# Layer 1 attention: the engines behind TensorE take the results of the projections two probability tiles later

## The reference

```python
xn = (x - mu) * rsqrt(var + EPS) * ln_g + ln_b
q = _split_heads(xn @ Wq)
kv = xn @ Wkv
k, v = _split_heads(kv[..., :INNER]), _split_heads(kv[..., INNER:])
mem = _split_heads(memories @ Wm)          # memories = the context
k = jnp.concatenate([k, mem], axis=2)
v = jnp.concatenate([v, mem], axis=2)
dots = jnp.einsum('bhid,bhjd->bhij', q, k) * scale
attn = jax.nn.softmax(dots, axis=-1)
out = jnp.einsum('bhij,bhjd->bhid', attn, v)
return out.transpose(0, 2, 1, 3).reshape(b, n, h * d) @ Wo + bo
```

## Time and profile before

| | us |
|---|---|
| median of 3 runs | 5270.39 |
| lowest and highest of them | 5267.61, 5272.48 |
| span of the profiled execution | 5269.8 |
| TensorE busy in it | 4827.1 |
| VectorE busy | 4327.4 |
| ScalarE busy | 3096.7 |
| GpSimd busy | 1940.9 |

### The profile page before, as it was taken

The page is one execution under the profiler, slowest core; times in us unless marked ns, Lnnn a source line. Parts: engine busy times, 40 slices in busy tenths (PEclk is TensorE's granted clock), DMA queues, the critical chain, the costliest instruction groups (busy, mean ns, idle before and its releaser), DMA issues. The chain is left out here.

```text
span 5269.8 us, 74714 instructions
## 1 busy us (share of the span) xinstructions
PE 4827.1 (92%) x26357; PEld 1891.5 (36%) x26366; DVE 4327.4 (82%) x4358; ACT 3096.7 (59%) x6111; POOL 1940.9 (37%) x1522
## 2 busy tenths in 40 slices
PE   8938999999999999999995699999998699999997
PEld 5623454544545454544442222222222322222222
DVE  7648878788787878878886699999996599999996
ACT  3313454454545454444442288888886288888886
POOL 0014878787787878787783100000000100000000
PEclk9968999999999999999997699999998699999998
DMA  1024334242333334142210211111110211111110
GB/s 36 5 89 117 95 92 112 60 124 51 103 81 98 98 82 122 40 123 64 51 38 15 78 29 29 29 34 29 29 23 2 78 28 29 28 29 33 30 23 6
DMA packets 171375, 298.10 MB, mean 57 GB/s; under 512 B 39061, under 2 KB 108577, under 8 KB 167393
## 3 DMA queue, kind: packets, MB, share of 16 engines
q1 hardware_dynamic: 169420, 292.95, 21.8%
q10 hardware_dynamic: 1584, 0.37, 0.0%
HBM read 187.39 MB, written 101.25 MB: 55 GB/s over the span
## 5 line engine op out<-in xcount | busy, mean ns | idle before, releaser
L1858 DVE TENSOR_REDUCE a_mx<-ps 128x1 f32<-128x1024 f32 x1536 | 1814.5, 1220 | 71.0 <-PE ps L1692 54.5
L1800 ACT ACTIVATE a_prob<-ps 128x512 f32<-128x512 f32 (+1 forms) x3264 | 1699.7, 601 | 288.1 <-PE ps L1680 283.3
L1227 POOL TENSOR_TENSOR tot_p<-tot_p,prob 128x512 f32<-128x512 f32 (+1 forms) x922 | 1300.4, 1410 | 401.5 <-ACT prob L1103 315.3
L1103 ACT ACTIVATE prob<-ps 128x512 f32<-128x512 f32 (+1 forms) x1512 | 801.1, 608 | 866.1 <-PE ps L979 865.2
L1151 DVE TENSOR_REDUCE mx<-ps 128x1 f32<-128x1024 f32 x896 | 1047.3, 1214 | 222.4 <-PE ps L956 222.4
L1692 PE MATMUL ps<-a_K,a_Q 59*128 59x512 bf16 (+1 forms) x3328 | 1094.7, 386 | 56.4 <-DMA a_Q<-q_stack_dram 44.5
L1680 PE MATMUL ps<-a_Q,a_K 59*128 59x512 bf16 (+1 forms) x3264 | 988.7, 383 | 55.8 <-ACT a_prob L1800 49.5
L1716 PE MATMUL ps<-a_prob,a_V 128*9 128x512 f32 x6528 | 871.8, 596 | 10.9 <-ACT a_acc L1784 10.9
L978 PE MATMUL ps<-QA,KA 128*128 128x512 f32 (+1 forms) x1888 | 841.7, 446 | 0.0
L990 PE MATMUL ps<-prob,V 128*64 128x512 f32 x3024 | 801.1, 599 | 0.7 <-ACT prob L1103 0.7
L979 PE MATMUL ps<-QB,KB 128*128 128x512 f32 (+1 forms) x1888 | 746.1, 395 | 0.0
(11 more groups left out here) (415 smaller groups left out, 3772.8 us busy)
## 6 DMA issues: line engine op xcount, KB each, us to landing
a_K<-k_stack_dram SPq DMA_DIRECT2D x128, 300.2 KB
k_hi_dram<-hi_s SPq DMA_DIRECT2D x112, 256.0 KB, 2.2
k_lo_dram<-lo_s SPq DMA_DIRECT2D x112, 256.0 KB, 2.4
KA<-k_hi_dram SPq DMA_DIRECT2D x64, 384.0 KB, 4.3
KA<-k_lo_dram SPq DMA_DIRECT2D x64, 384.0 KB, 5.6
KB<-k_hi_dram SPq DMA_DIRECT2D x64, 384.0 KB, 6.6
k_bf_dram<-bf_s SPq DMA_DIRECT2D x112, 128.0 KB, 1.8
KM<-k_bf_dram SPq DMA_DIRECT2D x32, 448.0 KB
```

The lines of the kernel that those rows point to most:

```text
L1103: nc.scalar.activation(prob_of(u, t)[0:r, :], c.banks(n % 3)[0:r, :], ACT.Exp, scale=SCALE).then_inc(exped, 1)
L1227: nc.gpsimd.tensor_tensor(tot_p[0:r, u % 2, :], tot_p[0:r, u % 2, :], p, ALU.add).then_inc(totalled_p, 1)
L1800: nc.scalar.activation(prob[0:r, batch % 2, t % BATCH, :], c.banks(n % 3)[0:r, :], ACT.Exp, scale=SCALE).then_inc(exped, 1)
L1858: nc.vector.tensor_reduce(mx[:, u % 2, j, i % FULL:i % FULL + 1], c.banks(slot(step), 2), AX.X, ALU.max).then_inc(maxed, 1)
```

## The change

A second constant says behind which score tile ScalarE, VectorE and GpSimd take an extra's result. TensorE and SyncE keep `EXTRAS_BEHIND`.

```diff
-    EXTRAS_BEHIND = (3, 5)
+    EXTRAS_BEHIND, TAKEN_BEHIND = (3, 5), (5, 7)
@@ block.scalar
                         for n, tile in enumerate(scored_in(u, r)):
                             exponential(*tile)
-                            if n in EXTRAS_BEHIND and extras:
+                            if n in TAKEN_BEHIND and extras:
                                 take_extra(*extras.pop(0))
```

## The result

The changed kernel takes 5445.48 us (median of 4 runs, 5442.41 to 5447.15) against 5271.43 us for the kernel before (4 runs): a ratio of 1.033, with a 95% interval of 1.0316 to 1.0345. It is 174 us slower. The forecast was 5421.5 us in a range of 5388 to 5460.

The account below looks back on a forecast made before the run. TensorE was taken to bound layer 1; stalls of 81.8 + 48.7 + 8.1 + 7.0 + 5.5 = 151.1 us on the 5269.8 us span, with 0.6 for the runs' median, gave 5421.5 us, range 5388 to 5460.

Parts of the forecast that it names:

- What bounds the kernel: Layer 1 goes at TensorE's pace: time added to its queue adds to the end; ScalarE has room.
- Two k: 56 rounds with two key projections: second maximum step of part 1 starts 1.46 us late, 81.8 us in all.
- The chain of the second step: Two-k rounds: exponentials 6 and 7, then `round_hi`, `cut_lo`, TensorE's second maximum step at 772.31 instead of 770.85.
- Two v: 42 rounds with two v projections: ScalarE's `take_v` alone releases the slot; stall 1.16 us each, 48.7 us in all.
- A fin and a v: 7 rounds with a fin, then a v behind n = 7: stall 1.16 us each, 8.1 us in all.
- One k: 7 rounds with one k, taken behind n = 5 instead of n = 3: 1.0 us each, 7 us in all.
- Fin alone: 24 rounds with only a fin: ScalarE's later `take_fin` delays TensorE's last pair 0.23 us each, 5.5 us in all.
- nothing wins it back: No TensorE work queued behind the waiting maximum step can slip past, so each stall is paid in full.
- No gain: ScalarE no longer waits for projections between exponentials, but exponential 6 starts with its score either way: no gain taken.
- That rival's 5447 us: VectorE's sum of n = 6 waits out another GpSimd sum in one k round in three: adds 26 us; chance 0.12.
- the clock: TensorE's clock falls behind the new stalls, 105 rounds' weighing at half clock: adds 389 us, 5811 us; chance 0.03.
- signs of being wrong: Second step not held, VectorE sums holding `cut_lo` in most rounds, or layer 1's granted clock under 1.

Follow-up runs that it names:

- the fill: Changed kernel with the first maximum step of part 1 issued six times in rounds with two k, keeping TensorE busy through the wait: 5414.90 us.
- ScalarE alone late: Changed kernel, but only ScalarE takes extras behind n = 5 and 7; VectorE and GpSimd as in the kernel before: 5434.96 us.
- the split kernel: Second maximum step of part 1 put behind the weighing's first four tiles: changed kernel 5311.41 us; the kernel before with the same edit 5288.00 us.
- VectorE and GpSimd alone late: Changed kernel, but only VectorE and GpSimd take extras behind n = 5 and 7; ScalarE as in the kernel before: 5347.45 us.
- k alone late: Changed kernel, but only k extras are taken two tiles later; v and fin as in the kernel before: 5389.62 us.

## Why the prediction was right, and where it was off

*What bounds the kernel: right.* ScalarE, VectorE and GpSimd all got more idle time, and the time followed TensorE's queue. Rounds without extras kept 9.22 us in every kernel of the table.

*Two k: right, with one part missing.* Worked out were 1.46 us of stall; with the clock held up by the fill, these rounds are 1.48 us longer, 83 us in all against 81.8. The chain of the second step was right link by link, and ScalarE is its longest part, as the run with ScalarE alone late shows. What it left out is the first step's wait of 0.22 us, which is hidden here but was the larger part of what the split kernel still lost.

*Two v: mis-sized.* 1.16 us was forecast, 1.00 measured (42 against 48.7 us). The step most at fault is the 0.14 us from the release to TensorE's start, borrowed from `cut_lo`. After `take_v` it is 0.05, which is 0.09 of the 0.16 us. TensorE and ScalarE in one round:

```profile
711.26 0.39 PE L956 MATMUL ps<-KM,QM 64*128 64x512 bf16 x2
712.51 0.39 PE L956 MATMUL ps<-KM,QM 64*128 64x512 bf16 x2 [0.87 <-ACT V L1063]
```

```profile
710.90 1.08 ACT L1103 ACTIVATE prob<-ps 128x512 f32<-128x512 f32 x2 [0.26 <-PE ps L979]
711.87 0.59 ACT L1063 COPY V<-ps 128x512 f32<-128x512 f32 x1
```

`take_v` ends at 711.87 + 0.59 = 712.46, and TensorE starts at 712.51. Of the rest, 0.03 us is that the two exponentials start that much sooner (0.36 us ahead of the first step, 710.90 to 711.26, in place of 0.33); and in seven of the 42 rounds the steps of part 1 stood 0.3 us later to begin with, so they lose 0.73 us and pull the mean down. The waits listed for `take_v` came to 35.0 and 5.4 us where some 50 were forecast. A fin and a v came to 0.94 against 1.16 us.

*One k: right in size,* 0.99 against 1.0 us.

*Fin alone: right in size, by the wrong cause.* These rounds are 0.23 us longer, which is the figure of the prediction, but it ascribed it to ScalarE's later copy. With ScalarE alone late the second step of part 1 is indeed held, and the weighing starts 0.15 us later. Still the round is not longer. The four matmuls with which the next round begins show why, first in the kernel before, then with ScalarE alone late:

```profile
829.25 0.77 PE L956 MATMUL ps<-KM,QM 64*128 64x512 bf16 x4
...
859.01 0.62 PE L956 MATMUL ps<-KM,QM 64*128 64x512 bf16 x4
```

Before, they took 0.77 us, because the second pair had to wait for a maximum on VectorE: in both kernels it starts 0.15 us behind the end of one. That wait swallows the late weighing. So "nothing wins it back" does not hold in these rounds. With VectorE and GpSimd alone late, that maximum itself comes later. GpSimd, VectorE and TensorE, first before (no wait of TensorE is listed), then in that kernel:

```profile
825.19 1.48 POOL L1242 TENSOR_TENSOR fin_s<-fin_s,rec 128x512 f32<-128x512 f32 x1
824.44 2.78 DVE L1173 TENSOR_TENSOR tot_d<-tot_d,prob 128x512 f32<-128x512 f32 x2 [0.83 <-ACT prob L1103]
...
840.25 2.98 POOL L1227 TENSOR_TENSOR tot_p<-tot_p,prob 128x512 f32<-128x512 f32 x2
842.20 1.58 DVE L1173 TENSOR_TENSOR tot_d<-tot_d,prob 128x512 f32<-128x512 f32 x1
846.19 0.39 PE L956 MATMUL ps<-KM,QM 64*128 64x512 bf16 x2 [0.23 <-DVE mx L1151]
```

VectorE's sum of n = 6 ends at 827.22, 0.55 us behind GpSimd's instruction (826.67), and at 843.78, again 0.55 behind GpSimd's (843.23). This 0.55 stands in all 23 full rounds of this kind, in these two kernels as in the changed one and the one with ScalarE alone late, and the sum takes 1.58 us here where the one of the earlier trace rows took 0.68. It points to GpSimd's order, in which a sum now stands ahead of the work for the fin and ends some 0.2 us later. No run moved GpSimd alone, so this is argued and not shown.

*No gain: right.* Scores waited 102.9 us for exponentials, as before (103.3).

*The rivals.* In rounds with two k the sum on VectorE did not wait out a sum of GpSimd: it took 0.73 us, 0.03 behind its exponential. That rival's 5447 us is near the measured time by chance. The rival that came true in part is the clock. It was priced for 105 rounds and for a whole weighing at half clock, 389 us; the runs show it in 17 rounds, with 1.69 us each, 29 us. That the clock could fall in some rounds only was the gap in the forecast: its chance of 0.03 was for all or nothing. One of the prediction's own signs of being wrong, a granted clock in layer 1 under 1, did appear (0.99). The time is inside the range in spite of it, because the range had room for a rival that did not happen. That part is luck.

The rounds' differences are 56 x 1.98 + 42 x 1.00 + 7 x 0.99 + 7 x 0.94 + 24 x 0.23 = 171.9 us, of 174.2 in the span. The 24 us by which the time lies above the forecast are 29 for the clock, minus some 8 for the v terms, and 3 us that the rounds don't account for; layer 1 itself ends 172 us later, so 2 of them lie behind it.

## What to carry to other kernels

When two engines pass a buffer back and forth, ask when the reader lets it go and what stands ahead of that in the reader's queue, then what stands right behind the waiting instruction in the writer's. Here ScalarE was idle for half of the time, and taking its copies later by some 1 us still cost the bound engine 1 to 1.5 us a round, since the weighing that was ready stood behind the waiting step. The remedy is in the order too: to issue and take the result one tile sooner won 28 us here. Ready work ahead of the step that waits has a price: it won 134 us where the wait was long, and lost 14 in the kernel before, where it was short.

## What was not expected of the hardware

A wait of TensorE can cost more than its length. In the changed kernel 49 weighings stand behind a wait of 1.40 us (a wait of 0.2 us stands ahead of the first step as well). Of these 17 took 1.69 us longer, each at a mean granted clock of 0.68. It was 16 of 49 with k alone late and 14 of 49 with ScalarE alone late. Behind waits of 1.30, 1.07 and 0.87 us, in other kernels here, none did, and none did when repeated matmuls filled the wait of 1.40. Why some and not all 49 stays open, and so does whether a wait of 1.4 us in a round with v would do the same, which no run here shows.

Going back and forth between maximum steps and weighing has a price of its own: 0.26 us in rounds with two v of the split kernels, which wait for nothing there.
